# In-chunk scores as 64x64 blocks, the angle net padded to 128 rows, and VectorE's pairs of instructions joined, in a Mamba-like mixer with experts

## Chip, cores, metric

One core of a Trainium2 chip. The metric is the device time of one execution in microseconds (us), the median of the runs shown. All arithmetic is fp32. A run can be told from no change here when it differs by more than about 0.2%.

## What is computed

Input `x` is 8 sequences of 1024 tokens with 256 features. It is normalised (LayerNorm), and the result feeds a mixer and a layer of 8 experts (each token goes to one); both outputs are added to `x`. The mixer is a state-space scan with complex decay in chunks of tokens, cut to what matters here:

```python
theta = clip(theta_base + tanh(x @ theta_w1) @ theta_w2, -pi/2, pi/2)      # the "angle net"
lambda_eff = lambda_base + viscosity_eta * theta ** 2
log_z = complex(-lambda_eff * dt, theta * dt)                              # per head and state block
cumlog = cumsum(log_z, axis=1)                                             # within a chunk
A = where(t >= s, exp(cumlog[t] - cumlog[s]), 0)
S_total = exp(cumlog) * state + einsum('btshk,bshp->bthpk', A * B, x * dt)
y = einsum('bthk,bthpk->bthp', C, S_total).real                            # + x * D, gate, RMS norm, out projection
```

## The kernel before

A first part (to about 225 us) normalises, routes tokens to experts and runs the experts. The rest, which the change is about, is the mixer: `whole_mixer`, 32 macros of 256 tokens (`MACROS`, `MT`), each of 2 tiles of 128 tokens (`TPM`, index `ch`); a tile holds two chunks of 64 (`CH`). Four macros make one sequence.

The loops are unrolled, and the order of the work on each engine is written out by hand: each engine has one list of steps that runs three to five macros of `front_*` work (projections, angles, waves) ahead of the `back_*` work (scores, state, output). Engines meet through semaphores (`s["name"]`) only; each engine works its own list in order. The steps named later:

- TensorE: `front_x` and `front_z_a/b` project tokens through `project` (L900; `front_x` runs in even macros for two macros at once, 32 records in a row and 8 more); `front_theta` (L926) is the second layer of the angle net, K = 49 rows (48 hidden and a row of ones); `back_own` (L980) makes the scores of a tile, for 4 pairs `q` of heads and 2 heads `e` in a pair, each a block of 128x128 with K = 64; `back_cross` (L992) then overwrites the block that goes from the first chunk to the second, 64x64; `back_update` (L1005), `back_y_att` (L1016), `back_y_state` (L1027), `back_turn` and `front_turn` (L968, L956, transposes), `back_out` (L1036), `back_square_sum` (L1044).
- ScalarE: copies of projections from PSUM (`front_x`, L1130 and L1131), `front_lambda` (L1145, L1148), exponentials and sines, scaling of waves, seeds and copies for the back.
- VectorE: `front_conv` (L1380), `front_clip` (L1387, clips theta on its way out of PSUM), `front_angle`, `front_phase`, `front_decay` (L1418, a scan for each of 2 groups of 256 columns), `front_cin` (L1443, L1444) and `front_cown` (L1456, L1457), products of the replicated B or C rows with a wave, `back_mask` (L1477, causal mask on the scores of a tile), `back_state` (L1488), `back_gate` (L1498).

An fp32 matmul call shows as two MATMUL records in the trace, a transpose as one. A form such as 64*128 in a record is rows times columns of the array that the instruction takes.

## Time and profile before

| | |
|---|---|
| time, median of 3 runs | 1089.71 us (1088.63 to 1090.44) |
| profiled execution, span of its instructions | 1074.8 us (the profile states no other time of this execution) |
| TensorE matmul busy | 977.5 us, 91% |
| VectorE busy | 923.2 us, 86% |
| ScalarE busy | 853.5 us, 79% |
| GpSimd busy | 347.3 us, 32% |
| chain that ended last | TensorE 63%, ScalarE 7% |

The shares are of the whole span; the mixer's steady part is read from windows of its own. The median of the runs lies 14.9 us above the profiled span, time that the profile's instructions do not cover.

### The profile page before, as it was taken

The numbers are of one execution on the slowest core, as the hardware profiler recorded it, in microseconds if no ns is written. First come the engines' busy times: TensorE is split into PE (matmuls) and PEld (weight loads), VectorE is DVE, ScalarE is ACT, GpSimd is POOL, SyncE is SP. The second block draws the span as 40 slices with busy tenths as digits, with TensorE's granted clock in tenths as the row PEclk, the third lists the DMA queues.
The fourth block names the chain that finished last, engine by engine and source line by source line (L and its number), as shares of the span: only waits on it lengthen the run. The fifth ranks groups of instructions, "written<-read, shape, count | busy, mean of one in ns | idle before, by whom it ended". The sixth has DMA issues, their size and how long they took to land.

```text
span 1074.8 us, 25050 instructions
## 1 busy us (share of the span) xinstructions
PE 977.5 (91%) x8702; PEld 803.8 (75%) x8702; DVE 923.2 (86%) x1487; ACT 853.5 (79%) x1771; POOL 347.3 (32%) x347
## 2 busy tenths in 40 slices
PE   4972699876899999999999999999999999999995
PEld 2532477655688888888888888888888888888884
DVE  5859723259999999999999999999999999999971
ACT  3864212139789999999999999999999999999982
POOL 1210677400213343323222332322333333222332
PEclk9985699996899999999999999999999999999998
DMA  7969587614364665657575656656665657575662
GB/s 244 312 218 394 165 256 208 164 49 155 114 172 142 187 169 165 183 157 200 147 212 149 191 156 191 160 184 186 175 178 164 184 156 202 147 216 136 172 189 58
DMA packets 145986, 193.72 MB, mean 180 GB/s; under 512 B 16862, under 2 KB 106127, under 8 KB 144448
## 3 DMA queue, kind: packets, MB, share of 16 engines
q1 hardware_dynamic: 110656, 146.68, 41.0%
q0 software_dynamic: 24672, 34.36, 16.7%
q10 hardware_dynamic: 10528, 11.01, 3.0%
q8 instruction: 73, 1.20, 0.5%
q14 instruction: 57, 0.47, 0.1%
HBM read 75.99 MB, written 40.63 MB: 109 GB/s over the span
## 4 chain that ended last, share of the span: by engine, by line
PE 63%; ACT 7%; issue 4%; DVE 2%; POOL 2%; DMA 1%; ACTq 0%; POOLq 0%; DVEq 0%
PE ps L900 20%; PE ps L1036 9%; PE ps L980 6%; PE ps L1016 5%; PE ps L1027 5%; PE ps L1044 4%; PE ps L992 3%; PE ps L1005 3%; PE ps L968 3%; PE ps L956 3%; PE ps L926 2%; DVE conv L1380 1%; POOL plus_tile L1590 1%; ACT ps L1166 1%; DMA plus_tile<-x 1%
## 5 line engine op out<-in xcount | busy, mean ns | idle before, releaser
L900 PE MATMUL ps<-early,win 128*128 128x256 f32 x1152 | 275.2, 389 | 11.0 <-DVE theta L1387 6.8
L900 PEld LDWEIGHTS ps<-early,win 128*128 128x128 f32 x1152 | 213.9, 193 | 45.9 <-DVE theta L1387 7.2
L1380 DVE SCALAR_TENSOR_TENSOR conv<-x_pre,col,conv 128x512 f32<-128x512 f32 x240 | 162.6, 741 | 6.4 <-ACT conv L1131 6.3
L1590 POOL DMA_INDIRECT plus_tile<-expert_d,slot_of x64 | 95.7, 1495 | 170.2 <-DMA out<-plus_tile 100.8
L1612 POOL TENSOR_TENSOR rms<-ms,cst 128x1 f32<-128x1 f32 x64 | 52.0, 812 | 250.6 <-ACT ms L1244 250.5
L1036 PE MATMUL ps<-wout,g 128*128 128x256 f32 x512 | 122.9, 383 | 2.5 <-ACT o_tile L1253 2.2
L1036 PEld LDWEIGHTS ps<-wout,g 128*128 128x128 f32 x512 | 93.4, 190 | 18.9 <-issue 7.8
L1596 POOL DMA_DIRECT2D plus_tile<-x x64 | 60.9, 956 | 101.9 <-ACT plus_tile L1237 101.9
L551 POOL DMA_INDIRECT r_tiles<-xn_d,token_of x72 | 68.7, 954 | 71.1 <-POOLq L408 48.5
L1605 POOL DMA_DIRECT2D plus_tile<-o_tile x62 | 67.4, 1092 | 54.6 <-ACT o_tile L1253 42.6
L682 DVE TENSOR_TENSOR r_tiles<-ps,r_expw 128x256 f32<-128x256 f32 x72 | 25.5, 416 | 65.9 <-PE ps L569 63.0
L1477 DVE TENSOR_TENSOR att<-ps,cst 128x1024 f32<-128x1024 f32 x64 | 77.8, 1216 | 4.5 <-PE ps L992 4.5
L603 ACT ACTIVATE r_tiles<-ps 128x1024 f32<-128x1024 f32 x18 | 18.4, 1024 | 76.5 <-PE ps L560 76.5
L1166 ACT ACTIVATE ps<-xbc,col 128x128 f32<-128x128 f32 x256 | 79.2, 364 | 0.0
L1130 ACT ACTIVATE x_pre<-ps 128x512 f32<-128x512 f32 x80 | 47.7, 597 | 39.0 <-PE ps L900 38.9
L569 PE MATMUL ps<-r_expw,r_tiles 128*128 x288 | 71.7, 398 | 4.7 <-issue 4.5
L980 PE MATMUL ps<-cown_s,grow_s 64*128 64x128 f32 x1024 | 75.3, 287 | 0.0
L980 PEld LDWEIGHTS ps<-cown_s,grow_s 64*128 64x128 f32 x1024 | 62.9, 189 | 16.4 <-issue 15.3
L1016 PE MATMUL ps<-att,x_tok 128*64 128x128 f32 x1024 | 70.9, 281 | 3.4 <-DVE att L1477 3.4
L1027 PE MATMUL ps<-cin_s,state_in 64*64 64x128 f32 x1024 | 70.6, 277 | 0.0
L1044 PEld LDWEIGHTS ps<-cst,gsq 128*128 128x128 f32 x512 | 67.2, 192 | 3.3
L569 PEld LDWEIGHTS ps<-r_expw,r_tiles 128*128 128x128 f32 x288 | 53.4, 196 | 20.2 <-issue 14.1
(172 smaller groups left out, 2237.3 us busy)
## 6 DMA issues: line engine op xcount, KB each, us to landing
cin_s<-cin SPq DMA_DIRECT2D x64, 258.0 KB, 3.1
rep<-bc_d SPq DMA_DIRECT2D x128, 128.0 KB, 3.3
grow_s<-grow SPq DMA_DIRECT2D x64, 256.0 KB, 3.8
bup_s<-bup SPq DMA_DIRECT2D x64, 256.0 KB, 3.0
cown_s<-cown SPq DMA_DIRECT2D x64, 256.0 KB, 2.7
expert_d<-r_tiles ACTq DMA_DIRECT2D x18, 512.0 KB, 3.4
xn_d<-r_tokens SPq DMA_DIRECT2D x16, 512.0 KB, 4.3
xnT_d<-r_turned SPq DMA_DIRECT2D x4, 2048.0 KB, 24.1
```

The costliest lines, as they stand in the source:

```text
L551: pool.indirect_dma_start(e_in[b][:, t, :], None, xn_d, bass.IndirectOffsetOnAxis(ap=token_of[:, at:at + 1], axis=0)).then_inc(e_loaded[b] ...
L569: last = nc.tensor.matmul(e_Y[b][:, t // 2, (t % 2) * D_MODEL:(t % 2 + 1) * D_MODEL], e_xT[b][:, kt, t * P:(t + 1) * P], w8[:, bass.ds(e + ...
L900: last = nc.tensor.matmul(dst, win[:, kt, n * P:(n + 1) * P], xn_in[b][:, kt, :], start=(kt == 0), stop=(kt == KT - 1))
L980: last = nc.tensor.matmul(bank_s[:, e, q * P:(q + 1) * P], grow_s[b][both(e), place(q), here], cown_s[b][both(e), place(q), here], start=T ...
L1016: nc.tensor.matmul(bank_y[both(e), q * P:(q + 1) * P], x_tok[b][:, ch, own], att[ch][:, e * PAIRS + q, :], start=False, stop=False, skip_g ...
L1027: last = nc.tensor.matmul(bank_y[both(e), q * P:(q + 1) * P], state_in[ch][both(e), place(q), :], cin_s[b][both(e), place(q), here], start ...
L1036: nc.tensor.matmul(bank_o[:, 0:D_MODEL], g[ch][:, q, :], wout[:, q, :], start=(q == 0), stop=(q == PAIRS - 1))
L1044: last = nc.tensor.matmul(bank_o[:, D_MODEL:D_MODEL + 1], gsq[:, q, :], k("ones")[:, 0:1], start=(q == 0), stop=(q == PAIRS - 1))
L1166: last = nc.scalar.activation(bank_y[:, q * P:(q + 1) * P], xbc[m % XBC_BUFS][:, q, ch * P:(ch + 1) * P], ACT.Copy, scale=c("D", q))
L1380: nc.vector.scalar_tensor_tensor(conv[:, ct, :], x_pre[:, ct, tap:tap + PT], c("conv_w", ct * D_CONV + tap), conv[:, ct, :], ALU.mult, ALU ...
L1477: nc.vector.tensor_tensor(att[ch][:, :, :], bank_s[:, :, :].rearrange("p e (h t) -> p (e h) t", h=4), k("causal")[:, None, :].broadcast_to ...
L1590: pool.indirect_dma_start(plus_tile[m % 2][ch][:, :], None, expert_d, bass.IndirectOffsetOnAxis(ap=slot_of[:, t:t + 1], axis=0)).then_inc( ...
```

## The change

TensorE: `back_own` makes each chunk's own 64x64 block instead of a tile's whole 128x128 block: 16 calls with K = 64, 64 columns of weights and 64 moving columns, where there were 8 calls of 64x128x128. The quarter that nobody writes any more (second chunk to first) is zeroed once by a memset of VectorE before the mixer starts, and TensorE waits for it. Within a macro `back_update(m, 1)` moves ahead of `back_own(m + 1, 0)`. The angle net's weights get 79 rows of zeros, so that `front_theta` has K = 128. ScalarE gets a new step `front_theta_out` in each macro, which copies theta from PSUM to SBUF; `front_clip` then clips in SBUF. The two products of `front_cin` and of `front_cown` become one instruction each, the two scans of `front_decay` one.

```diff
-                    here = slice(ch * P, (ch + 1) * P)
+                    chunks = [slice(ch * P + n * CH, ch * P + (n + 1) * CH) for n in range(CPT)]
...
                     for q in range(PAIRS):
                         for e in range(2):
-                            last = nc.tensor.matmul(bank_s[:, e, q * P:(q + 1) * P], grow_s[b][both(e), place(q), here], cown_s[b][both(e), place(q), here], start=True, stop=True)
-                            if q == PAIRS - 1:
-                                last.then_inc(s["scored"], 1)
+                            for chunk, here in enumerate(chunks):
+                                last = nc.tensor.matmul(bank_s[both(chunk), e, q * P + chunk * CH:q * P + (chunk + 1) * CH], grow_s[b][both(e), place(q), here],
+                                                        cown_s[b][both(e), place(q), here], start=True, stop=True)
+                                if q == PAIRS - 1:
+                                    last.then_inc(s["scored"], 1)
...
-                pe.wait_ge(m_zero, 1)
+                pe.wait_ge(m_zero, 2)
...
                 for m in range(MACROS):
+                    back_update(m, 1)
                     back_own(m + 1, 0)
-                    back_update(m, 1)
...
+                def front_theta_out(m):
+                    after(act, s["lamsq"], m)
+                    after(act, s["angle"], m)
+                    act.wait_ge(s["thproj"], m + 1)
+                    nc.scalar.activation(theta[:, :, :], bank_b.rearrange("p (n t) -> p n t", n=GROUPS2), ACT.Copy).then_inc(theta_out, 1)
...
                     back_reseed(m + 2, 1)
+                    front_theta_out(m + 5)
                     front_x(m + 5, 4)
...
-                    after(dve, s["lamsq"], m)
-                    dve.wait_ge(s["thproj"], m + 1)
-                    nc.vector.tensor_scalar(theta[:, :, :], bank_b.rearrange("p (n t) -> p n t", n=GROUPS2), 0.25, -0.25, ALU.min, ALU.max).then_inc(s["clipped"], 1)
+                    dve.wait_ge(theta_out, m + 1)
+                    nc.vector.tensor_scalar(theta[:, :, :], theta[:, :, :], 0.25, -0.25, ALU.min, ALU.max).then_inc(s["clipped"], 1)
...
-                    for n in range(GROUPS2):
-                        nc.vector.tensor_tensor_scan(decay[:, n, :], k("restart"), lam[:, n, :], 0.0, ALU.mult, ALU.add).then_inc(s["rsum"], 1)
+                    flat = lam[:, :, :].rearrange("p g t -> p (g t)")
+                    nc.vector.tensor_tensor_scan(flat, k("restart"), flat, 0.0, ALU.mult, ALU.add).then_inc(s["rsum"], GROUPS2)
...
-                    nc.vector.tensor_tensor(prod[0][:, :, :, :], c_re, wave[:, :, :, :], ALU.mult).then_inc(s["cprod"], 1)
-                    nc.vector.tensor_tensor(prod[1][:, :, :, :], c_im, wave[:, :, :, :], ALU.mult).then_inc(s["cprod"], 1)
+                    waves = wave.rearrange("p r g t -> p (r g) t")[:, None, :, :].broadcast_to([P, 2, 2 * GROUPS2, MT])
+                    nc.vector.tensor_tensor(both_prods, c_rep, waves, ALU.mult).then_inc(s["cprod"], 2)
...
-                dve.wait_ge(m_zero, 1)
+                nc.vector.memset(bank_s[:, :, :], 0.0).then_inc(m_zero, 1)
+                dve.wait_ge(m_zero, 2)
```

`front_cown` changes as `front_cin` does; the waits of TensorE on `clipped` become waits on `theta_out`; `restart` is 512 columns wide instead of 256; the waits on `scored` count 6 for a tile instead of 4.

TensorE's list at the start of a macro's back, before (names are PSUM, weights and moving operands; `x8` is 8 calls):

```order
L900 MATMUL ps<-early,win 128x256 x4
L980 MATMUL ps<-cown_s,grow_s 128x128 x8
L1005 MATMUL ps<-x_tok,b_tok 64x64 x8
L992 MATMUL ps<-cin_s,bup_s 64x64 x8
L968 MATMUL ps<-cst,bup_s 128x128 x4
```

and the same place now:

```order
L902 MATMUL ps<-early,win 128x256 x4
L1009 MATMUL ps<-x_tok,b_tok 64x64 x8
L983 MATMUL ps<-cown_s,grow_s 64x64 x16
L996 MATMUL ps<-cin_s,bup_s 64x64 x8
L970 MATMUL ps<-cst,bup_s 128x128 x4
```

The scores of the chunks now stand beside the cross block, which has the same form of tile. ScalarE's list around the new copy (theta out of PSUM between the copy of the state and the last `front_x` column tile of an even macro), as it is now:

```order
L1156 ACTIVATE lam<-theta 128x512 [waits negd,expd,clipped]
L1159 ACTIVATE lam<-lam,col 128x256 [waits lamsq]
L1159 ACTIVATE lam<-lam,col 128x256
L1234 ACTIVATE ps<-state_in 128x256 [waits statein]
L1149 ACTIVATE theta<-ps 128x512 [waits thproj,angle,lamsq]
L1134 ACTIVATE x_pre<-ps 128x512 [waits xproj]
L1135 ACTIVATE conv<-ps,col 128x512
L1241 ACTIVATE b_tok<-ps 128x512 [waits upd,bturned]
```

Before, the row `theta<-ps` was not there, and the others followed in the same order. VectorE's list from the mask to the first scan, before:

```order
L1477 TENSOR_TENSOR att<-ps,cst 128x1024 [waits scored,yout]
L1402 TENSOR_TENSOR lam<-lam,early 128x512 [waits dt_loaded0,lamd]
L1387 TENSOR_SCALAR theta<-ps 128x512 [waits thproj,lamsq]
L1418 SCALAR_TENSOR_TENSOR lam<-cst,lam 128x256 [waits negd,expd,lamdt]
L1418 SCALAR_TENSOR_TENSOR lam<-cst,lam 128x256
L1395 TENSOR_TENSOR angle<-theta,early 128x512 [waits dt_loaded1,fracd,clipped]
```

and now, where the clip waits for ScalarE's copy (semaphore `cwave`, which is `theta_out`) and one scan stands for two:

```order
L1493 TENSOR_TENSOR att<-ps,cst 128x1024 [waits scored,yout]
L1418 TENSOR_TENSOR lam<-lam,early 128x512 [waits dt_loaded0,lamd]
L1403 TENSOR_SCALAR theta<-theta 128x512 [waits cwave]
L1434 SCALAR_TENSOR_TENSOR lam<-cst,lam 128x512 [waits expd,negd,lamdt]
L1411 TENSOR_TENSOR angle<-theta,early 128x512 [waits dt_loaded1,fracd,clipped]
```

The order of VectorE's steps is the same; each place has fewer rows.

## Rows read from the trace of the kernel before

**Rows 1.** Busy time of each engine by windows, clock and DMA

```profile
core 0: us, PE busy (x) PEld busy (x) DVE busy (x) ACT busy (x) POOL busy (x), PEclk, DMA share, GB/s
461.01:1015.08 554.07, 554.07 (x5458) 471.09 (x5458) 549.77 (x761) 524.68 (x1113) 174.66 (x176) 1.00 0.62 174
...
300.00:1041.00 741.00, 738.04 (x7316) 627.10 (x7312) 730.50 (x1005) 699.40 (x1489) 244.74 (x239) 1.00 0.62 174
225.00:300.00 75.00, 57.87 (x360) 46.25 (x361) 65.83 (x92) 59.05 (x104) 8.95 (x5) 0.82 0.32 106
1041.00:1064.00 23.00, 21.03 (x268) 18.48 (x268) 6.72 (x11) 9.14 (x24) 8.43 (x11) 1.00 0.44 110
```

**Rows 2.** The chain in order of time, two macros: start, length in us, piece

```profile
602.31 1.73 PE ps L900 x8
604.04 1.09 PE ps L980 x16
605.13 0.61 PE ps L1005 x16
605.74 0.61 PE ps L992 x16
...
609.46 1.02 PE ps L1016 x16
...
621.51 1.06 PE ps L926 x4
622.57 1.92 PE ps L900 x8
```

**Rows 3.** Waits from 461.01 to 1015.08: us in total, times, longest

```profile
ACT x_pre L1130 <- PE ps L900: 27.4, 33, 1.9
...
DVE g L1498 <- PE ps L1027: 4.3, 11, 0.5
```

**Rows 4.** VectorE groups by form, 461.01 to 1015.08: busy, mean ns, idle before

```profile
L1418 DVE TENSOR_TENSOR_SCAN lam<-cst,lam 128x256 f32<-128x256 f32 x44 | 27.7, 669 | 0.0
L1444 DVE TENSOR_TENSOR prod<-rep,wave 128x1024 f32<-128x1024 f32 x22 | 26.7, 1215 | 0.0
...
L1387 DVE TENSOR_SCALAR theta<-ps 128x512 f32<-128x512 f32 x22 | 15.0, 680 | 0.0
```

**Rows 5.** VectorE in order of time, steady part: start, length in us

```profile
608.00 1.22 DVE L1443 TENSOR_TENSOR prod<-rep,wave 128x1024 f32<-128x1024 f32 x1
609.13 1.22 DVE L1444 TENSOR_TENSOR prod<-rep,wave 128x1024 f32<-128x1024 f32 x1
610.27 0.68 DVE L1423 SCALAR_TENSOR_TENSOR frac<-frac,angle 128x512 f32<-128x512 f32 x1
```

**Rows 6.** VectorE groups by form, 60 to 130 us, the nearest to the new forms

```profile
L470 DVE TENSOR_TENSOR r_tokens<-r_tokens,r_route 128x2048 bf16<-128x2048 f32 x4 | 9.1, 2282 | 0.0
...
L446 DVE TENSOR_TENSOR_SCAN r_route<-cst,early 128x512 f32<-128x512 f32 x1 | 1.2, 1224 | 0.0
...
L641 DVE TENSOR_SCALAR early<-early 128x512 f32<-128x512 f32 x1 | 0.5, 489 | 0.8 <-ACT early L610 0.8
...
L642 DVE TENSOR_SCALAR early<-early 128x512 f32<-128x512 f32 x1 | 0.4, 426 | 0.0
```

**Rows 7.** ScalarE's copy of 512 columns from PSUM, groups by form, 461.01 to 1015.08

```profile
L1130 ACT ACTIVATE x_pre<-ps 128x512 f32<-128x512 f32 x55 | 32.8, 597 | 27.4 <-PE ps L900 27.4
```

**Rows 8.** Around theta's way out of PSUM, in order of time

```profile
623.80 0.37 ACT L1223 ACTIVATE ps<-state_in 128x256 f32<-128x256 f32 x1
...
626.04 0.68 DVE L1387 TENSOR_SCALAR theta<-ps 128x512 f32<-128x512 f32 x1
```

**Rows 9.** The mixer's start in order of time

```profile
224.37 0.27 DVE L1511 MEMSET state_in<- 128x256 f32 x1 [3.12 <-DMA expert_d<-r_tiles]
...
224.69 1.22 PE L1049 MATMUL ps<-state_in,cst 128*128 128x256 f32 x2
...
225.71 9.80 PE L900 MATMUL ps<-early,win 128*128 128x256 f32 x40
```

More of the change, by code:

```diff
@@ L43 @@
 CONST, _at = {}, 0
-for _n, _w in (("ident", P), ("minushalf", 8), ("causal", P), ("before", P), ("ones", P), ("restart", MT), ("tilestart", TILES * EXPERTS),
+for _n, _w in (("ident", P), ("minushalf", 8), ("causal", P), ("before", P), ("ones", P), ("restart", GROUPS2 * MT), ("tilestart", TILES * EXPERTS),
                ("first", EXPERTS), ("slot", SLOT_TILES), ("quarter", 1), ("halfpi", 1), ("eps", 1), ("ownhead", 2)):
@@ L101, in mixer_and_experts @@
         early_dt = [early[:, (XN_BUFS * KT + b * GROUPS2) * MT:(XN_BUFS * KT + (b + 1) * GROUPS2) * MT].rearrange("p (g t) -> p g t", g=GROUPS2) for b in range(2)]
-        early_hidden = [early_rows(XN_BUFS * KT + 2 * GROUPS2 + b, LORA + 1) for b in range(2)]
+        early_hidden = [early_rows(XN_BUFS * KT + 2 * GROUPS2 + b) for b in range(2)]
         passed = sem("passed")
@@ L672, in _ @@
                     for m in range(2):
-                        step(nc.vector.memset(early_hidden[m][32:LORA + 1, :], 1.0))
+                        step(nc.vector.memset(early_hidden[m], 1.0))
                     assert done[0] == ROUTE_READ
@@ L713, in whole_mixer @@
             trig, wave, grow, bpart, bup, cown = (wb(n, [P, 2, GROUPS2, MT]) for n in ("trig", "wave", "grow", "bpart", "bup", "cown"))
-            prod = [wb(f"prod{n}", [P, 2, GROUPS2, MT]) for n in range(2)]
+            prods = wb("prods", [P, 2, 2, GROUPS2, MT])
+            prod = [prods[:, n] for n in range(2)]
+            both_prods = prods.rearrange("p n r g t -> p n (r g) t")
             cin = wb("cin", [P, 2, GROUPS2, MT + TPM])
@@ L718, in whole_mixer @@
             rep = wb("rep", [P, 4, MT])
-            b_re, b_im, c_re, c_im = (rep[:, n:n + 1, None, :].broadcast_to([P, 2, GROUPS2, MT]) for n in range(4))
+            b_rep, c_rep = (rep[:, n:n + 2, None, :].broadcast_to([P, 2, 2 * GROUPS2, MT]) for n in (0, 2))
             hidden, xn_in, dt_in = early_hidden, early_xn, early_dt
@@ L738, in whole_mixer @@
             COPIES = 4 * 16
-            reseeded = s["wavedec"]
-            BEFORE = 4
+            reseeded, theta_out = s["wavedec"], s["cwave"]
+            SCORES = 6
             def place(q):
@@ L816, in stack_grow @@
                     b = m % 2
-                    after(sp, s["scored"], 8 * (m - 1))
+                    after(sp, s["scored"], TPM * SCORES * (m - 1))
                     sp.wait_ge(s["grown"], m + 1)
@@ L823, in stack_cin @@
                     b = m % 2
-                    after(sp, s["scored"], 8 * (m - 1))
+                    after(sp, s["scored"], TPM * SCORES * (m - 1))
                     after(sp, s["yout"], TPM * (m - 1))
@@ L833, in stack_bup @@
                     b = m % 2
-                    after(sp, s["scored"], 8 * (m - 1))
+                    after(sp, s["scored"], TPM * SCORES * (m - 1))
                     after(sp, s["bturned"], TPM * (m - 1))
@@ L841, in stack_cown @@
                     b = m % 2
-                    after(sp, s["scored"], 8 * (m - 1))
+                    after(sp, s["scored"], TPM * SCORES * (m - 1))
                     sp.wait_ge(s["cown"], 2 * (m + 1))
@@ L919, in front_theta @@
                     if m % 2:
-                        pe.wait_ge(s["clipped"], m)
+                        pe.wait_ge(theta_out, m)
                         after(pe, s["zevac"], 2 * (m - 1))
@@ L1138, in front_z @@
                     nc.scalar.activation(z_gate[b][:, 2 * h:2 * h + 2, :], (bank_a, bank_b)[h].rearrange("p (n t) -> p n t", n=2), ACT.Silu).then_inc(s["zevac"], 1)
+                @macro
+                def front_theta_out(m):
[3 more added lines that the diff above has]
+                    nc.scalar.activation(theta[:, :, :], bank_b.rearrange("p (n t) -> p n t", n=GROUPS2), ACT.Copy).then_inc(theta_out, 1)
                 @macro
@@ L1269, in scalar_mixer @@
                 front_x(0, 4)
+                front_theta_out(0)
                 front_z(0, 0)
                 front_lambda(0)
+                front_theta_out(1)
                 front_silu(0)
@@ L1295, in scalar_mixer @@
                 front_x(2, 4)
+                front_theta_out(2)
                 front_bpart(1, 1)
@@ L1308, in scalar_mixer @@
                 back_ms(0, 0)
+                front_theta_out(3)
                 front_trig(2)
@@ L1333, in scalar_mixer @@
                 back_b(1, 1)
+                front_theta_out(4)
                 front_x(4, 4)
```

14 lines of the change are left out of this document (7 added, 7 removed).

## Prediction

> **What bounds the kernel now.** I read the windows by stage first [rows 1]. From 461.01 to 1015.08 us, 11 repeats of a pair of macros and so 22 macros, TensorE is busy 554.07 of 554.07 us: 25.19 us a macro, at the full 2.4 GHz (granted clock 1.00). From 300 to 1041 it is busy 99.6%, with the same clock. So in these 741 us TensorE sets the pace, and the chain in order of time [rows 2] is one TensorE block behind another, with nothing between. Second, what the others need in the same 22 macros: VectorE 549.77 us (24.99 a macro), ScalarE 524.68 (23.85). The waits [rows 3] say where they stand idle: ScalarE 27.4 us before the copies of `front_x`, VectorE 4.3 before the gate, both for TensorE. VectorE is thus 0.2 us a macro behind the bound: whatever TensorE gains, VectorE lets through only 0.2 plus what it gains itself. That is the point on which the sum turns. Before 300 us and after 1041 VectorE and ScalarE are not full [rows 1].
>
> **TensorE, step by step.** Blocks in [rows 2] run from start to start, so they hold the cost of changing the form of tile. A projection of 8 records takes 1.73 us where the form before it is its own, 128*128, and 1.92 behind `front_theta`, whose form is 49*128; `front_theta` itself is 4 like records, so half of 1.73, 0.87, and takes 1.06. Entering and leaving costs 0.19 each time. With K = 128 its form is that of its neighbours: −0.38 a macro.
>
> `back_own` takes 1.09, `back_cross` 0.61. The length of a 64-column step follows from `back_y_att` (16 records, 128 moving columns, 1.02) against `back_update` (16 records, 64 columns, 0.61): 64 more columns cost 0.41 over 8 pairs of records, 0.051 a pair. So these tiles work two at a time, and a block of 8 pairs of 64 columns is 0.41, plus about 0.20 for the change of form. A projection of 256 columns at 0.216 a record gives 0.054 for 64 columns, the same step for a single tile.
>
> `back_own` now is 32 records of 64x64, in turn on the four quarters of the array. No row shows four quarters at once. Bounds: four at a time, 8 steps of 0.051, 0.41; two at a time, 0.82. Both pairings that it is built of are there: two row halves (`back_cross`) and two column halves (`back_update`) each reach 0.61 for 16 records, and nothing in the two looks like a limit that the other shares. I take 0.41, one step above the nearest rows, and keep 0.82. The block has the form of `back_cross` behind it, so the 0.20 is paid once for both. Own and cross together: 1.09 + 0.61 = 1.70 before, 0.41 + 0.61 = 1.02 now, −0.68, twice a macro −1.36 (two at a time: −0.54). The move of `back_update` is what puts own beside cross; it issues no DMA, and its own wait (copy of B, reseed) comes one block earlier, 1.09 us, where TensorE now never waits. TensorE needs 25.19 − 0.38 − 1.36 = 23.45 a macro (24.27 with two at a time).
>
> The Trainium skill, "TensorE: Matmul & The Clock Gate", section "Wait — 56ns, not 53.3ns?", says that matmuls never start less than about 25 ns apart however small they are. By it 32 records take 0.80 us, and the estimate for TensorE would be 24.2 us a macro instead of 23.45. The trace has a step of 0.051 for two records, so it neither reaches nor breaks that.
>
> **VectorE.** Records overlap: products follow each other at 1.13 and 1.14 us though each shows 1.22 [rows 5], so one costs its length less 0.08. The joined product has 2048 columns; the nearest row, 128x2048, is 2.28 [rows 6], so 2.20 against 2.27 for two: −0.07, and for both pairs −0.14. Bounds: no gain, if broadcasting reads cost something, and −0.16. Scans: two of 669 ns [rows 4] less the overlap are 1.18; one of 512 columns is 1224 ns [rows 6], 1.14: −0.04. Clip: 680 ns out of PSUM [rows 4]; in SBUF the rows with 512 columns are 426 and 489 ns [rows 6]: −0.25 or −0.19, I take −0.22. Sum −0.40: 24.99 becomes 24.59. It may be less, since "busy" counts short waits that lie under the overlap: up to 0.2 a macro, floor 24.4.
>
> **ScalarE.** One more copy of 512 columns out of PSUM, 597 ns [rows 7], 0.49 to 0.60 with and without the overlap: 23.85 becomes 24.34 to 24.45. Of its 27.4 us of waits, 1.25 a macro, nearly all stand in `front_x` and wait for TensorE, so they shrink as TensorE gets ahead. What is queued behind the copy: the last `front_x` evacuation, then `back_b`, the seed. The copy starts when the state copy before it is done: in the pair of [rows 2] that ends at 624.17 [rows 8], 1.6 us after `front_theta` (622.57), and VectorE reaches the clip at 626.04, 1.3 us after a copy of 0.6 would end. So I cost the new wait at nothing. If this cover went, each macro would lose up to the 0.6 of the copy.
>
> **Sum.** The slowest engine is VectorE with 24.59, ScalarE 0.15 to 0.25 behind, TensorE over 1 us ahead. I take a macro at 24.6: −0.59. The 741 us hold 29.4 macros: −17.3. Tail, TensorE busy 21.03 of 23.00 [rows 1], two tiles' scores: −1.4. Fill, 75 us, shared between three engines: −0.6 (0 to −2). Start: VectorE's new memset covers 1024 columns of PSUM; no such memset is there, one of 256 in SBUF takes 0.27 [rows 9], so 1.1, and TensorE's first projections wait for it since they start right after the first memset: +1.1 (0.5 to 1.3). Wider constants and weight rows: +0.3 (0 to 0.7). Together −17.9: span 1074.8 to 1056.9, and with the 14.9 us outside it (1089.71 − 1074.8) the median goes to 1071.8, say **1072**.
>
> **Rivals.**
> - *The quarters go two at a time, or by the 25 ns of the page.* TensorE then needs 24.2 to 24.3, all three engines lie within 0.35 of each other, and each one's waits cost the others: 24.75 a macro, −12.9 in the steady part, 1076. For it: no row has four at once. Against: the two pairings.
> - *Three engines full, poorly coupled.* VectorE 24.6 and ScalarE 24.4 wait for each other (exponentials to waves to scaling, convolution to SiLU to seed): a macro at 24.9 to 25.1, 1079 to 1087. For: between them only 0.15 to 0.25 us a macro is left, and both stand at 99% of such a period. Against: VectorE at 99% of TensorE's time costs TensorE nothing today.
> - *ScalarE becomes the bound and the kernel slower.* Its place: the copy ahead of the last `front_x` evacuation. If its present idle time stayed as it is (29.4 of 554 us, 1.34 a macro), it would need 23.85 + 0.5 + 1.34 = 25.7: +0.5 a macro, +15, about 1103. It decides from 0.85 us of idle that stays. Against: that idle time is waiting for TensorE.
> - *The quarters don't overlap at all*: 32 records at 0.051, 1.63, own and cross 2.24, +1.08 − 0.38 a macro: TensorE 25.9, 1110. Against: every form with two tiles overlaps.
> - *It does nothing*: VectorE's savings don't come (broadcast reads slow the joined products, the clip stays 0.6): period 24.9 to 25.1 again, at most −5.
>
> **Chances.** Forecast 0.55, with a range of its own from 1064 (VectorE at its floor 24.4: −23.2 − 1.4 − 2 + 1.1) to 1076; two at a time 0.15; poor coupling 0.15; nothing 0.05; ScalarE 0.06; no overlap 0.03; the small rest to both sides. The range goes to 1084, which takes in the second case and most of the third. Faster by over 0.2% (about what a measurement tells here) 0.87, within 0.2% 0.05, slower 0.08.
>
> **What would show it.** Own blocks of 32 records in about 0.41 to 0.45 us (0.8: two at a time), and 0.61 for cross behind them. `front_theta` 0.87 and 1.73 for what follows. TensorE idle for over 0.8 us a macro, waiting for masks, gates or copies of VectorE and ScalarE, and VectorE at 99% busy. Joined product near 2.28, scan 1.22, clip 0.43 to 0.49. The distance of two long projections, 50.37 us now for a pair of macros, at 49.2. ScalarE's waits in `front_x` down from 1.25 a macro to below 0.5. Clock 1.00: if TensorE's new gaps took it to 1.2 GHz for a stretch, or if ScalarE's list stood idle for VectorE and not for TensorE, the prediction is wrong.

## The result, and the profile after

The changed kernel takes **1097.93 us** (1097.24 to 1099.45) against 1089.76 us of the kernel before (four runs; the 1089.71 of the table further down is the median of three): a ratio of **1.0077, interval 1.0063 to 1.0092**. It is slower by 0.8%, where 1.6% faster was forecast. In short, the experiments below show two things: ScalarE, with the new copy in its list, sets the pace of the changed kernel, and once that copy is gone a VectorE without pauses holds up GpSimd's small operations, for which ScalarE waits.

The profiled execution took 1098.01 us with a span of 1096.2, so only 1.8 us lie outside the span. The page of after, its engines and the first line of its chain:

```profile
span 1096.2 us, 27099 instructions
...
PE 949.4 (87%) x9726; PEld 774.2 (71%) x9726; DVE 912.9 (83%) x1392; ACT 867.8 (79%) x1803; POOL 379.8 (35%) x347
...
ACT 41%; PE 16%; issue 16%; POOL 10%; DVE 3%; DMA 1%; another core or an unknown queue 1%; ACTq 1%; POOLq 0%; DVEq 0%
```

The chain has left TensorE. The windows that answer to [rows 1] (PE, PEld, DVE, ACT, POOL busy, clock, DMA share, GB/s):

```profile
461.01:1015.08 554.07, 531.15 (x6156) 451.17 (x6155) 541.56 (x693) 533.48 (x1133) 203.49 (x176) 1.00 0.63 175
...
225.00:300.00 75.00, 50.39 (x278) 39.11 (x278) 51.93 (x73) 44.64 (x79) 2.95 (x4) 0.82 0.29 90
1041.00:1064.00 23.00, 20.54 (x278) 17.77 (x278) 18.40 (x20) 21.28 (x51) 9.67 (x10) 1.00 0.74 199
```

In the steady part no engine is full now: TensorE idles 22.9 us, VectorE 12.5, ScalarE 20.6. The two later windows lie at other places of the program than in [rows 1], since everything runs later. GpSimd has gone up from 174.66 to 203.49 us with the same 176 instructions; the experiments come back to that.

The parts themselves came out nearly as costed. TensorE in order of time (start, length); what a block costs is the distance to the next start:

```profile
740.62 0.69 PE L983 MATMUL ps<-cown_s,grow_s 64*64 64x64 f32 x32
741.14 0.64 PE L996 MATMUL ps<-cin_s,bup_s 64*64 64x64 f32 x16
741.71 0.66 PE L970 MATMUL ps<-cst,bup_s 128*128 128x128 f32 x4
...
743.46 1.89 PE L902 MATMUL ps<-early,win 128*128 128x256 f32 x8
745.18 1.89 PE L1040 MATMUL ps<-wout,g 128*128 128x256 f32 x8
...
755.04 0.69 PE L983 MATMUL ps<-cown_s,grow_s 64*64 64x64 f32 x32
```

Own scores 0.52 and cross 0.57, 1.09 together where [rows 2] add up to 1.70; the projection behind the padded angle net 1.72 instead of 1.92. The four quarters do overlap: 32 records in 0.52 us are 16 ns apart on average. TensorE's busy time, 531.15 us or 24.1 a macro, is above the 23.6 that its blocks add up to with these lengths; some of them are longer behind a wait (the output projection 1.80 in the median instead of 1.73 from start to start), and the rest of the difference is not followed here. VectorE's and ScalarE's new forms in the steady part (busy, mean ns), which answer to [rows 4, 6, 7]:

```profile
L1460 DVE TENSOR_TENSOR prods<-rep,wave 128x2048 f32<-128x2048 f32 x22 | 50.2, 2282 | 0.0
...
L1434 DVE TENSOR_TENSOR_SCAN lam<-cst,lam 128x512 f32<-128x512 f32 x22 | 26.8, 1217 | 0.0
...
L1149 ACT ACTIVATE theta<-ps 128x512 f32<-128x512 f32 x22 | 12.7, 575 | 0.0
...
L1403 DVE TENSOR_SCALAR theta<-theta 128x512 f32<-128x512 f32 x22 | 9.2, 420 | 0.0
```

VectorE needs 541.56 / 22 = 24.62 us a macro (24.59 forecast; the window still holds 22 macros to within 0.2%, one pair of them a long one). All of this is close to the forecast, and yet the distance between two 32-record projections (`front_x` for ct 0 and 1, the clock of a pair of macros) fell only from 50.37 to 50.28 us. The waits say who held it. The third line is what the first of [rows 3] has become:

```profile
POOL rms L1629 <- ACT ms L1255: 168.2, 43, 6.7
...
PEld ps L1040 <- issue: 24.0, 32, 2.4
...
ACT x_pre L1134 <- PE ps L902: 17.0, 21, 1.6
PE ps L1040 <- ACT o_tile L1264: 15.5, 32, 2.1
```

TensorE waits at the output projection (L1040) for ScalarE's `o_tile`, the scaled output, and ScalarE, behind that, for the first `front_x` projection. So the two wait for each other in turn, a closed chain. The chain in order of time shows it; ScalarE works through some 40 us without a wait for another engine, of which the end is:

```profile
824.08 0.47 issue
...
826.30 1.28 ACT L1142
827.64 0.16 issue
827.90 0.19 issue
828.09 0.48 ACT o_tile L1264
828.70 1.97 PE ps L1040 x8
830.66 0.79 PE ps L1048 x8
831.45 1.06 PE ps L1020 x16
832.51 1.02 PE ps L1031 x16
833.53 0.61 PE ps L1009 x16
834.14 1.06 PE ps L902 x4
```

From the end of `o_tile` it is 5.6 us until TensorE starts the projection that ScalarE needs next, and meanwhile ScalarE runs out of work.

### The profile page after: what moved, and what is told of

Its sections match the earlier page's. It is cut to its first block, busy times and chain, and to the rows that moved or that the text cites. A ratio compares the mean times of both kernels' runs of the same rounds, so it can differ in the third digit from the quotient of the medians.

```text
span 1096.2 us, 27099 instructions
## 1 busy us (share of the span) xinstructions
PE 949.4 (87%) x9726; PEld 774.2 (71%) x9726; DVE 912.9 (83%) x1392; ACT 867.8 (79%) x1803; POOL 379.8 (35%) x347
## 4 chain that ended last, share of the span: by engine, by line
ACT 41%; PE 16%; issue 16%; POOL 10%; DVE 3%; DMA 1%; another core or an unknown queue 1%; ACTq 1%; POOLq 0%; DVEq 0%
POOL r_tiles L551 6%; PE ps L902 5%; ACT ps L1177 4%; ACT bup L1225 3%; PE ps L1040 3%; ACT L1142 3%; ACT conv L1135 3%; ACT L1210 2%; ACT x_tok L1186 2%; ACT bpart L1225 2%; PE ps L1020 2%; ACT plus_tile L1248 2%; ACT x_pre L1134 2%; ACT o_tile L1264 2%; PE ps L1031 2%
## 5 line engine op out<-in xcount | busy, mean ns | idle before, releaser
L902 PEld LDWEIGHTS ps<-early,win 128*128 128x128 f32 x1152 | 216.5, 194 | 43.6 <-DMA early<-xnT_d 5.7
L1607 POOL DMA_INDIRECT plus_tile<-expert_d,slot_of x64 | 110.4, 1726 | 162.1 <-DMA out<-plus_tile 85.0
L1629 POOL TENSOR_TENSOR rms<-ms,cst 128x1 f32<-128x1 f32 x64 | 69.6, 1088 | 239.6 <-ACT ms L1255 239.5
L1040 PE MATMUL ps<-wout,g 128*128 128x256 f32 x512 | 126.0, 389 | 27.0 <-ACT o_tile L1264 26.8
L1040 PEld LDWEIGHTS ps<-wout,g 128*128 128x128 f32 x512 | 94.2, 192 | 49.5 <-issue 38.1
L551 POOL DMA_INDIRECT r_tiles<-xn_d,token_of x72 | 69.0, 958 | 85.0 <-POOLq L408 48.5
L682 DVE TENSOR_TENSOR r_tiles<-ps,r_expw 128x256 f32<-128x256 f32 x72 | 25.5, 418 | 78.2 <-remote 50.2
L569 PE MATMUL ps<-r_expw,r_tiles 128*128 x288 | 74.4, 400 | 13.7 <-issue 12.1
L569 PEld LDWEIGHTS ps<-r_expw,r_tiles 128*128 128x128 f32 x288 | 49.2, 190 | 36.7 <-issue 33.0
L1460 DVE TENSOR_TENSOR prods<-rep,wave 128x2048 f32<-128x2048 f32 x32 | 73.1, 2284 | 0.0
L1473 DVE TENSOR_TENSOR prods<-rep,cin 128x2048 f32<-128x2048 f32 x32 | 73.0, 2282 | 0.0
```

Source lines behind the costliest of these rows:

```text
L551: pool.indirect_dma_start(e_in[b][:, t, :], None, xn_d, bass.IndirectOffsetOnAxis(ap=token_of[:, at:at + 1], axis=0)).then_inc(e_loaded[b] ...
L569: last = nc.tensor.matmul(e_Y[b][:, t // 2, (t % 2) * D_MODEL:(t % 2 + 1) * D_MODEL], e_xT[b][:, kt, t * P:(t + 1) * P], w8[:, bass.ds(e + ...
L902: last = nc.tensor.matmul(dst, win[:, kt, n * P:(n + 1) * P], xn_in[b][:, kt, :], start=(kt == 0), stop=(kt == KT - 1))
L1040: nc.tensor.matmul(bank_o[:, 0:D_MODEL], g[ch][:, q, :], wout[:, q, :], start=(q == 0), stop=(q == PAIRS - 1))
L1460: nc.vector.tensor_tensor(both_prods, c_rep, waves, ALU.mult).then_inc(s["cprod"], 2)
L1473: nc.vector.tensor_tensor(both_prods, b_rep, rotated, ALU.mult).then_inc(s["bprod"], 2)
```

## The experiments

There are fourteen runs beside the two kernels: the changed kernel once more (c1) and thirteen variants. Chips differ: the kernel before takes 1075.8 to 1076.7 us on four of them, and 1089 to 1090 in the first measurement and on one chip later, so ratios are each to the kernel before measured beside the run. The table gives them with the distances between the starts of the 32-record projections, read from TensorE's timeline: the intervals 2, 3 and 4 (the fill, in which the engines' lists are only getting under way; interval 1 lies between 29.6 us in e2 and 33.7 in e3 and isn't shown), then the usual later interval, and the longer ones. The intervals are those of the one profiled execution, while the times are medians, and where long pairs come and go the two can differ: e1's executions run from 1070.48 to 1084.96 us with 1083.62 profiled, e3's from 1063.92 to 1078.41 with 1073.84, e8's from 1069.40 to 1080.45 with 1069.50.

| kernel | us | ratio [interval] | intervals 2, 3, 4 | steady | longer ones |
|---|---|---|---|---|---|
| before | 1089.71 | 1 | 48.4, 52.0, 52.0 | 50.37 | none |
| changed | 1097.93 | 1.0077 [1.0063, 1.0092] | 55.4, 53.2, 52.0 | 50.28 | 52.09 |
| c1 changed again | 1085.15 | 1.0081 [1.0065, 1.0098] | 54.9, 53.3, 52.0 | 50.29 | 52.08 |
| e1 no copy | 1077.26 | 1.0009 [0.9983, 1.0035] | 45.8, 53.0, 49.3 | 49.31 | 53.86, three of 54.95 |
| e2 copy alone | 1084.64 | 1.0077 [1.0061, 1.0093] | 56.6, 52.2, 52.2 | 50.37 | 52.15 |
| e3 TensorE's part alone | 1076.81 | 0.9992 [0.9969, 1.0014] | 45.9, 49.1, 50.0 | 49.88 | 57.17 |
| e4 VectorE's joins alone | 1076.82 | 1.001 [1.0001, 1.002] | 48.5, 53.0, 51.8 | 50.37 | none |
| e5 changed, theta 2 early | 1080.86 | 1.0041 [1.0026, 1.0055] | 50.2, 53.2, 52.0 | 50.29 | 53.74 |
| e6 e1 + 2 memsets | 1068.37 | 0.993 [0.9916, 0.9943] | 46.9, 49.0, 49.6 | 49.55 | 55.93 |
| e7 e1 + 4 memsets | 1062.78 | 0.9866 [0.9849, 0.9882] | 45.9, 49.0, 49.8 | 49.65 | 53.55 |
| e8 e5 + 4 memsets | 1072.42 | 0.9975 [0.9956, 0.9995] | 48.6, 49.9, 50.3 | 50.29 | none |
| e9 before + 4 memsets | 1075.5 | 0.999 [0.9973, 1.0007] | 50.1, 52.1, 50.4 | 50.37 | none |
| e10 e3 + 4 memsets | 1071.38 | 0.9942 [0.9919, 0.9964] | 46.0, 49.0, 50.2 | 50.0 | 55.49 |
| e11 e7 + 2 memsets | 1075.59 | 0.987 [0.9852, 0.9888] | 45.6, 53.1, 49.3 | 49.68 | none |
| e12 e8, ScalarE relieved | 1072.9 | 0.985 [0.9836, 0.9864] | 49.7, 49.3, 49.4 | 49.42 | none |
| e13 e7 + 2 others | 1061.59 | 0.9863 [0.9839, 0.9886] | 45.7, 49.0, 49.7 | 49.7 | none |

### The change taken apart: e1 to e4

e1 is the changed kernel with the theta copy undone; e2 to e4 each put one part alone into the kernel before.

```diff
 # e1, against the changed kernel
 def front_clip(m):
-    dve.wait_ge(theta_out, m + 1)
-    nc.vector.tensor_scalar(theta, theta, 0.25, -0.25, ALU.min, ALU.max)
+    after(dve, s["lamsq"], m)
+    dve.wait_ge(s["thproj"], m + 1)
+    nc.vector.tensor_scalar(theta, bank_b, 0.25, -0.25, ALU.min, ALU.max)
 # and no front_theta_out in ScalarE's list; TensorE waits for s["clipped"] again
 # e2: before + copy. e3: before + 64x64 own, padding, moved update, bank memset.
 # e4: before + joined products and scan
```

> The changed kernel without ScalarE's copy of theta: VectorE clips out of PSUM again, the rest of the change stays. Theory (a closed chain through ScalarE and TensorE sets the steady period, and the copy is what filled it): the distance of two 32-record projections falls from 50.28 us to 49.0 to 49.5, ScalarE's busy time in 22 macros falls by 10 to 13 us, and the time is 1084 to 1090 us. Rival (the copy is hidden, and something else of the change holds the period, VectorE or the order of TensorE): distance stays at 50.2 to 50.4, time 1097 to 1100. In both, the mixer's start (the first 40-record projection) shows whether the later start of the changed kernel belongs to the copy: neither theory says so, so 237 to 239 us.

> The kernel before with ScalarE's copy of theta and the clip in SBUF alone. Theory: TensorE still needs 25.19 us a macro, ScalarE's chain gets 0.48 us a macro longer and just reaches it: distance 50.3 to 50.9, time 1090 to 1102 us. Rival (the copy is hidden in ScalarE's wait for TensorE): distance 50.37 unchanged and 1088 to 1091 us.

> The kernel before with TensorE's part alone: own scores as 64x64 blocks, the angle net padded, the state update moved ahead, the memset of the bank. Theory: ScalarE's chain is as before and has about 1 us a pair of slack, VectorE needs 49.98 us a pair: distance 49.9 to 50.1, steady part 3 to 5 us shorter, time 1086 to 1091. Rival (the move of the state update or the mixed tile forms make TensorE wait anew): distance 50.3 or more, time above 1092. If the late start of the mixer comes with this part (128-row weights and memset of the angle net's tiles), it shows here at about 238 us, otherwise at about 226.

> The kernel before with VectorE's joined products and scan alone. Theory: VectorE is 0.2 us a macro behind the bound, so no gain in the steady part (distance 50.37), 1088 to 1091 us. Rival (a joined instruction ends later than the first of a pair did, and the waves, copies or exponentials behind it wait): distance over 50.5, time above 1093.

The copy alone costs as much as the whole change (e2: 1.0077, the change: 1.0077), but taking it away gives no gain either (e1: 1.0009), although its steady distance is **49.31 us, where 49.2 was forecast**. Of e2 the theory had the size right and the place wrong: its distance stays 50.37, as the rival said, and 5.2 us are lost in the fill (its third long projection starts at 311.75 us instead of 306.53). e3 has 49.88 with VectorE at 544.8 of 545 us, as expected, but one pair of 57.17. e4 gains nothing, as expected. So two things take the gain away: something in the fill that belongs to the copy, and single long pairs that appear when the copy is gone.

**The long pairs.** In e1 TensorE and ScalarE both wait in such a pair. ScalarE waits for GpSimd's power (`back_rms`, which raises the mean square of each token to a power for the norm: one element per partition). From 606 to 623 us, GpSimd:

```profile
606.13 3.31 POOL L1595 DMA_INDIRECT plus_tile<-expert_d,slot_of  x1 [0.30 <-issue]
611.44 9.65 POOL L1617 TENSOR_TENSOR rms<-ms,cst 128x1 f32<-128x1 f32 x1 [2.00 <-ACT ms L1248]
622.29 0.93 POOL L1601 DMA_DIRECT2D plus_tile<-x  x1 [1.20 <-ACT plus_tile L1241]
```

and VectorE beside it:

```profile
611.17 0.46 DVE L1492 TENSOR_TENSOR state_in<-ps,cin_s 128x256 f32<-128x256 f32 x1
611.51 0.72 DVE L1467 TENSOR_TENSOR cown<-prods 128x512 f32<-128x512 f32 x1
612.11 0.73 DVE L1468 TENSOR_TENSOR cown<-prods 128x512 f32<-128x512 f32 x1
612.71 4.10 DVE L1384 SCALAR_TENSOR_TENSOR conv<-x_pre,col,conv 128x512 f32<-128x512 f32 x6
616.68 0.73 DVE L1473 TENSOR_TENSOR bup<-bup,bpart 128x512 f32<-128x512 f32 x1
617.28 0.73 DVE L1474 TENSOR_TENSOR bup<-bup,bpart 128x512 f32<-128x512 f32 x1
617.88 2.78 DVE L1384 SCALAR_TENSOR_TENSOR conv<-x_pre,col,conv 128x512 f32<-128x512 f32 x4
620.53 1.26 DVE L1481 TENSOR_TENSOR att<-ps,cst 128x1024 f32<-128x1024 f32 x1
```

The power takes 0.55 us where nothing holds it up. Here it takes 9.65 and ends 0.56 us after the mask has started, which is its normal length from there on. Between lie 14 VectorE instructions in 9.0 us, every one with two SBUF inputs, back to back; the mask is the first that has one of its two from PSUM. In e3 the same stretch holds up one of GpSimd's gathers (an indirect DMA that it issues to fetch a tile's expert rows), 9.74 us instead of 1.1, and ScalarE waits 7.5 us for its rows:

```profile
407.91 9.74 POOL L1594 DMA_INDIRECT plus_tile<-expert_d,slot_of  x1 [0.18 <-issue]
```

It ends 1.06 us after the mask starts (416.59), again its normal length. I call this a lockout. It is no novelty of the change: in the trace of before a gather issued at 384.78 us, in the fill, takes 4.83 and ends 0.97 after the start of the gate (388.64), which reads PSUM; the pair around it takes 52.0 us.

The Trainium skill, "SBUF — State Buffer", section "SBUF: two separate sides", says that a VectorE instruction with two SBUF inputs and a GpSimd instruction that reads SBUF exclude each other on a shared port pair, the one that starts first keeping it for its whole instruction while the other is blocked. The traces fit that, and go further: the block lasted over 14 instructions, not one, and the same instructions held up gathers too.

### The fill, and the chip: c1 and e5

Where is the time of the fill lost? In the trace of after, ScalarE and then VectorE around the copy for macro 2:

```profile
285.20 0.57 ACT L1241 ACTIVATE b_tok<-ps 128x512 f32<-128x512 f32 x1
286.59 0.60 ACT L1241 ACTIVATE b_tok<-ps 128x512 f32<-128x512 f32 x1 [0.81 <-PE ps L970]
287.08 0.59 ACT L1134 ACTIVATE x_pre<-ps 128x512 f32<-128x512 f32 x1
287.56 0.78 ACT L1135 ACTIVATE conv<-ps,col 128x512 f32<-128x512 f32 x1
288.22 0.61 ACT L1149 ACTIVATE theta<-ps 128x512 f32<-128x512 f32 x1
```

```profile
281.17 2.72 DVE L1397 SCALAR_TENSOR_TENSOR conv<-x_pre,col,conv 128x512 f32<-128x512 f32 x4
288.86 0.43 DVE L1403 TENSOR_SCALAR theta<-theta 128x512 f32<-128x512 f32 x1 [4.97 <-ACT theta L1149]
```

TensorE's product, theta of macro 2, is there at 282.7. ScalarE does exponentials, two B copies and a `front_x` evacuation first, VectorE waits 4.97 us, and behind the waiting clip stand the waves of macro 1 and the first mask, for which TensorE waits. e5 moves the one line; c1 is the changed kernel unaltered. Both ran on the same chip.

```diff
                 front_trig(1)
+                front_theta_out(2)
                 front_exp(1)
                 back_b(0, 0)
                 back_b(0, 1)
                 front_x(2, 4)
-                front_theta_out(2)
```

> The changed kernel once more, unaltered, beside the others on their chip. On another chip the kernel before took 1075.8 us where it had taken 1089.7, and the trace of the changed kernel came from the slower one. Theory (the mixer's start at 237.99 us instead of 225.71 belongs to that chip and its expert stage, not to the change): here the first 40-record projection starts at 224 to 227 us if this chip is the faster kind, and the ratio to the kernel before is again 1.006 to 1.009. Rival (the late start belongs to the change, through its wider weights or its code): 237 us whatever the chip, and a ratio of 1.015 or more on a fast chip.

> The changed kernel with one line of ScalarE's list moved: in the fill the copy of theta for macro 2 stands ahead of the exponentials of macro 1 instead of behind them, two B copies and the last front_x. Theory (the loss is in the fill: VectorE's clip waits 5.0 us for this copy, with the waves of macro 1 and the first mask queued behind it): the second interval of the 32-record projections shrinks from 55.35 to about 50 us, the steady part stays at 50.28, and the time is 4 to 6 us below that of the changed kernel, within 2 us of the kernel before or up to 0.2% under it. Rival (the wait is covered, ScalarE is late anyway): under 1 us less than the changed kernel.

e5: interval 2 goes from 54.86 to 50.17 and the time is 4.3 us down, as the theory said; but it stays 4.9 us above the kernel before, where at most 2 had been expected. In c1 the mixer's first projections start here:

```profile
227.15 1.06 PE L902 MATMUL ps<-early,win 128*128 128x256 f32 x2
```

against 237.99 in the first trace of the same code: those 11 us are not the change's but the chip's. From the first memset to this projection it is 2.47 us (224.68 to 227.15), in [rows 9] 1.34: the memset of the bank, 0.91 us, costs 1.1. The other 0.3 us by which c1 starts later lie ahead of it, where executions differ anyway (e5 has the same memset and starts at 223.75).

### GpSimd let in: e6, e7, e9, e10

If the block is VectorE's unbroken run, an instruction without SBUF inputs inside it should end it. These kernels add memsets of one column to VectorE's list (`open_port`), which write a tile that nobody reads.

```diff
+def open_port(m):
+    nc.vector.memset(port[:, opened.pop()], 0.0)     # a new column each time
 # in VectorE's loop over m
     front_cin(m + 2)
+    open_port(m)          # e7 to e13 only
     front_frac(m + 3)
     ...
     front_conv(m + 4, 0, 6)
+    open_port(m)
     front_bup(m + 2)
     back_join(m, 1)
+    open_port(m)
     front_conv(m + 4, 6, 10)
     ...
     front_decay(m + 3)
+    open_port(m)          # e7 to e13 only
```

> The changed kernel without ScalarE's copy (as in the first experiment), plus two memsets of one column that VectorE does inside its run of state, sums, convolution and B products. In the first experiment the distance of two long projections was 49.31 us, as forecast, but every third pair took 54.95, and in these GpSimd's power for the norm, a single element per partition, took 9.65 us: from the start of that run of VectorE instructions with two SBUF operands to the first one that reads PSUM, the mask. Theory (VectorE, never idle now, locks GpSimd out while it runs instructions with two SBUF operands back to back; an instruction with none lets it in): the power never takes over 5.3 us, the 54.95 us pairs are gone or cost under 2 us, distance 49.4, time 1058 to 1066 us where the kernel before takes 1075.8. Rival 1 (one column is too short to let GpSimd in): the power still takes 9.6 us and the time stays at 1070 to 1085. Rival 2 (the long power is only a symptom and the stall has another cause, a late transfer): the powers get shorter and the 54.95 us pairs stay.

> As the port-gap experiment, with two more one-column memsets of VectorE in each macro: behind the scan, ahead of the last five steps of the convolution, and behind the joined product of C, ahead of the fractions. With two memsets the power once took 5.65 us (the run of scan, convolution, angle) and a gather 5.1 and 3.3, and that pair was 55.93 us long. Theory (lockout, ended by any instruction without two SBUF operands): no power or gather above 4.5 us, all pairs 49.3 to 49.7, time 1060 to 1064 us beside 1075.9. Rival (the stall that is left is not from the lockout): one or two pairs of 55 us stay, time 1067 to 1070.

> The kernel before with the four one-column memsets a macro and nothing else, as a control. Theory (before, TensorE is the bound and VectorE's own waits let GpSimd in): distance 50.37, time within 0.15% of the kernel before. Rival (the memsets or the openings help by themselves, and the gain of the port-gap experiment isn't the change's): over 2 us faster.

> The kernel before with TensorE's part (64x64 own blocks, padded angle net, update moved ahead, memset of the bank) and the four memsets, without VectorE's joins and without ScalarE's copy. Alone, that part had a steady distance of 49.88 us (VectorE busy 544.8 of 545 us) and no gain: in its trace a gather of GpSimd's took 9.74 us and the pair with it 57.17. Theory: the long pairs go, the steady distance stays at 49.8 to 49.9 (VectorE's need without the joins), 1063 to 1067 us. Rival (lockout isn't what cost it): a pair of 55 us or more stays and the time is above 1071.

By the ratios e6 is 0.79%, 8.5 us, faster than e1, to which it adds the memsets alone; its 1068.37 us miss the 1058 to 1066 that had been expected. The 9.65 us powers are gone; the first two memsets don't lie in the run of scan, convolution and angle, and there a power still takes long, over its bound of 5.3:

```profile
666.62 5.65 POOL L1625 TENSOR_TENSOR rms<-ms,cst 128x1 f32<-128x1 f32 x1 [3.37 <-ACT ms L1250]
672.45 5.12 POOL L1603 DMA_INDIRECT plus_tile<-expert_d,slot_of  x1 [0.18 <-issue]
```

It ends 0.5 us after the gate (which reads PSUM) starts at 671.77, with the 55.93 us pair behind it. With four memsets (e7) no power of the mixer takes over 1.7 us (two gathers, at 286.06 and 424.55 us, still take 5.96 and 4.97, where 4.5 was the bound) and the time is **1062.78, ratio 0.9866**. Its steady part is the one that was forecast, with VectorE as the bound. Its row for 461 to 1000 us:

```profile
461.00:1000.00 539.00, 521.86 (x6095) 445.82 (x6093) 539.00 (x774) 519.97 (x1100) 193.45 (x175) 1.00 0.63 176
```

The price of the memsets is 49.65 − 49.31 = 0.34 us a pair for eight. The control e9 shows that they give the kernel before nothing that this measurement can tell: there TensorE is the bound. e10 gains 0.6%, but its median and the pair of 55.49 in its profiled execution are what the rival named. In that pair a gather takes 7.10 us, from 410.12: it starts behind the state's product, runs through the first, unopened part of the stretch above, isn't ended by the memset at 414.99, and ends 1.0 us behind the one at 416.21. So it looks like the same block, in a part of the list where the memsets came too late, and one memset isn't sure to let a gather in.

### ScalarE's part in the steady distance: e8 and e12

> The whole changed kernel (ScalarE's copy of theta included), with the copy for macro 2 moved ahead in the fill and the four one-column memsets a macro. Theory: the copy keeps ScalarE's closed chain at 50.28 us a pair, so the memsets save only the one long pair (1.8 to 3.5 us): distance 50.28, no pair above 51, 1077 to 1079 us. Rival (GpSimd's lockout, and not ScalarE's list, holds the steady pair at 50.28): distance 49.5 to 49.9 and 1066 to 1072 us.

> The changed kernel with its copy, with the early theta copy and the four memsets, and ScalarE relieved at another place: its scaling of the gathered expert rows covers one column instead of 256 (so the gate is left out of the other 255 columns), twice a macro, some 0.25 us less each, 1.0 us a pair. Theory (ScalarE's list, a closed chain with TensorE's projections, holds the pair at 50.29 us): the distance falls to 49.4 to 49.7, to VectorE's need, and the time by 6 to 9 us against 1072.4. Rival (not ScalarE's load but the new dependence holds it, projection to copy to clip, or the freeing of the bank): distance stays at 50.2 to 50.3, time within 2 us of 1072.4.

```diff
 # e12, against e8
-nc.scalar.activation(tile[:, :], tile[:, :], ACT.Copy, scale=gate[:, t:t + 1])
+nc.scalar.activation(tile[:, 0:1], tile[:, 0:1], ACT.Copy, scale=gate[:, t:t + 1])
```

e12 leaves out the gate for 255 of the 256 columns, so its output is not the mixer's: it serves to weigh ScalarE's list and is no version to use.

e8: the distance stays at 50.29, so GpSimd doesn't hold the changed kernel's steady pair. I had expected the memsets to save one long pair only; by the ratios (1.0041 to 0.9975) they saved 0.66%, 7.1 us, against e5, and intervals 3 and 4 of the fill (53.24 and 52.0) also fell, to 49.94 and 50.30. Those look like lockouts as well: in e5 these two hold a gather of 4.33 us and three powers of 2.35 to 2.53, in e8 none of the powers takes over 1.2 and no gather over 2.6. But the profiled execution of e8 is one of its fastest, so the median may hold long pairs that the table doesn't show.

e12 makes ScalarE's four scalings a pair shorter (minimum, median and maximum in ns, e8 and then e12):

```profile
L1250 ACT ACTIVATE plus_tile<-plus_tile,gate x44: 500/512/538, 463.2 to 995.4; 128x256 f32<-128x256 f32 x44
L1250 ACT ACTIVATE plus_tile<-plus_tile,gate x43: 281/298/326, 477.3 to 993.6; 128x1 f32<-128x1 f32 x43
```

That is 4 x 0.214 = 0.86 us, and the distance falls by 50.29 − 49.42 = 0.87. Copy and dependences are the same, and in e8 none of these scalings waits for its rows. **ScalarE's list sets the changed kernel's pair.** That the two agree to 0.01 us says less than it seems, since VectorE is at 99.5% in e12 and would soon have stopped the fall. The time fell by more than the 6 to 9 us that were expected: 1.25% by the ratios, 13 us, of which the shorter pairs explain some 11. The row of e12, from 475 to 1011 us:

```profile
475.00:1011.00 536.00, 522.49 (x6114) 444.65 (x6112) 533.56 (x772) 518.65 (x1120) 175.09 (x175) 1.00 0.63 178
```

### The last long pair: e11 and e13

```diff
 # e11, against e7: inside the convolution
-front_conv(m + 4, 0, 6)
+front_conv(m + 4, 0, 3); open_port(m); front_conv(m + 4, 3, 6)
-front_conv(m + 4, 10, 15)
+front_conv(m + 4, 10, 13); open_port(m); front_conv(m + 4, 13, 15)
 # e13, against e7: between gate, phase and waves
     back_gate(m + 1, 1)
+    open_port(m)
     front_phase(m + 4)
+    open_port(m)
     front_waves(m + 3)
```

> The version with four memsets and without the copy, with two more: inside the first six steps of the convolution and inside its last five. What was left there: one pair of 53.55 us in the fill, where a gather took 4.97 us and the power behind it was late. Theory (lockout): no pair above 51 us, steady distance 49.7 (0.1 more for four memsets a pair of 0.03 to 0.05 each), time 1059 to 1062 where the four-memset version has 1062.8. Rival (the late gather has another cause, its queue or its transfer): the 53 us pair stays and the time is 1063.

> The version with four memsets and without the copy, with two more memsets in the one long run that neither it nor the six-memset version opened: between the gate and the phase scan, and between the phase scan and the waves. In the traces of both, the one long pair that was left (53.55 and 53.09 us) has a late GpSimd instruction exactly there: a gather of 4.97 us that ends 1 us behind the start of the mask, and a power of 3.03 us that ends 0.5 us behind it. Theory (lockout): no pair above 51.5 us, time 3 to 4 us below the four-memset version less 1 us for the memsets: a ratio to the kernel before of 0.983 to 0.985 where that version has 0.9866. Rival (that pair is long for the ramp of the fill, and GpSimd's late instruction only falls into it): the 53 us pair stays, ratio 0.987.

e11 opened the wrong run: a pair of 53.09 us stays, with a power of 3.03 us between gate and mask, where no memset stood, and the ratio is e7's. e13 opens that run, and in its profiled execution no pair is above 49.89 us and no power above 1.7. But its median ratio, 0.9863, can't be told from 0.9866, and 0.983 to 0.985 had been expected. That the last long pair is a lockout is likely from where it stands and from its absence in e13; what it is worth in the median stays open.

e13 and e7 are faster than both kernels: 1.3 to 1.4% under the kernel before, 2.1% under the changed one by the ratios.

## Why the prediction was wrong, point by point

Between the kernel before (1075.92) and the changed one (1085.15) lie 9.2 us on one chip. From the starts in c1 and in the trace of before, whose profiled execution was of the same kind of chip: start +1.4, interval 1 −1.7, interval 2 +6.4, interval 3 +1.3, steady −0.8, one long pair +1.7, tail +0.4; together 8.7. The forecast had −17.3 for the steady part, and its −0.8 is the larger share of the miss: there ScalarE's list holds the pair (e8, e12), and where the copy is gone, GpSimd's lockout takes back what the shorter pair gains (e1, e6, e7). Behind the plus signs the experiments put two causes: the place of one copy in the fill (4.3 us, e5) and the lockout (7.1 us, e8 against e5). The two needn't add up to 9.2, since the kernel before has lockouts in its fill too, and the memsets take away more than the change brought. With both mended the change is worth −0.25%; without the copy and with GpSimd let in, −1.34%, 14.4 us.

- **TensorE, own and cross 1.02: 1.09 measured**, mis-sized by 0.07. The rival of two at a time falls with 16 ns a record. So does the floor of 25 ns in the Trainium skill, "TensorE: Matmul & The Clock Gate", section "Wait — 56ns, not 53.3ns?", for records on different quarters of the array. `front_theta` came close to its cost: 0.97 us behind a short wait, 0.87 without one (in e7), and 1.72 for what follows.
- **VectorE 24.59 a macro: 24.62 measured.** Products and scan came within 10 ns of the rows chosen for them, the clip at 420 ns where 460 was taken.
- **"I cost the new wait at nothing": the first step that failed.** The cover, the time by which the copy is done before VectorE gets to the clip, was read at one place, in the steady part (1.3 us there), and not in the fill, which has a list of its own. There the clip waits 4.97 us with waves and mask behind it, and moving that one copy gives back 4.3 us (e5).
- **"They shrink as TensorE gets ahead": the second, and the one that cost the steady gain.** ScalarE's waits for projections went from 27.4 to 17.0 us, 0.77 a macro where below 0.5 was forecast, and 20.6 / 22 = 0.94 us a macro of idle time stayed. The rival "ScalarE becomes the bound" named the copy, and a point of decision at 0.85 us of idle that stays: 24.25 busy + 0.94 idle = 25.19. It had 6 in 100. It had the engine right, but not the price or the place: the idle it was to keep whole (1.34) shrank by a third, so the steady pair didn't get longer, and the loss against the kernel before lies in the fill. What the prediction missed is that waiting for TensorE can itself be a result of ScalarE's lateness: TensorE waited at L1040 for `o_tile`. That only shows when the chain is followed around. The experiments bear it out: with ScalarE's list 0.86 us shorter the pair is 0.87 shorter (e12), and without the copy it is 49.31 (e1).
- **Not in any rival: GpSimd.** The sum compared three engines that were to be full at once and left out the fourth, 32% busy. A full VectorE locks it out, and ScalarE waits for it: 9.65 us instead of 0.55 in e1, and its pair takes 54.95 instead of 49.31. The rival "three engines full, poorly coupled" had the right symptom and the wrong place. This is also why e1, whose steady distance came out within 0.1 us of the forecast, gained nothing.
- **The base.** I took 14.9 us as lying outside the span, from a median of 1089.71 and a span of 1074.8. Each run here is its span plus 1.8 us; so the trace of before, with its 1074.8, must be of a faster kind of chip than the median (its mixer starts at 225.71 us, as those of the faster chips do). That didn't change the sign of the forecast, but the 14.9 us are no time outside a span.
- **Start +1.1: right.** From the first memset to the first long projection it is 1.1 us more (2.47 against 1.34). **Tail −1.4: +0.4 measured**; what took it was not tested.

## What to carry to other kernels

When the bound is taken away and VectorE gets full, look at who lives in VectorE's pauses. Here GpSimd's small operations and its gathers needed one, and four one-column memsets a macro between VectorE's instructions with two SBUF inputs cost 0.04 us each and were worth 1.4% (e1 to e7). An engine's idle time is free only if the wait behind it isn't caused by that engine itself: follow the chain once around before loading it. And where the fill has a list of its own, an operation moved to another engine has to be placed there by itself, counting what is queued behind its reader.

## What was not expected of the hardware

- GpSimd's one-element power, 0.55 us, took 9.65 us beside 14 VectorE instructions with two SBUF inputs, and ended 0.5 to 0.6 us after the first instruction with an input from PSUM began (three cases: 9.65 us in e1, 5.65 in e6 and 3.03 in e11). Gathers of 9.74 us in e3, 4.97 in e7 and 4.83 in the kernel before ended 1.0 to 1.1 us after such a start. Memsets of 0.06 us, which have no input, took most of these blocks away (e6, e7), though not each of them ended one (e10). Not every power in such a run was held for all of it: in e1 one issued at 562.13 us took 1.56. What lets it in there is open, and so is why only every third pair was struck. Powers of 1.3 to 1.9 us stand in many pairs, in the kernel before too (1.35 us in most of its pairs).
- Lateness can multiply: in the long pair of c1 TensorE waited 2.06 us for `o_tile`, the granted clock of 600 to 605 us was 0.76, so part of it at 1.2 GHz, and the output projection behind the wait took 3.65 us instead of 1.97.
- The same code took about 1076 us on some chips and 1089 on others, the changed kernel 1085.15 and 1097.93. Of these 12.8 us 10.8 lie ahead of the mixer, which starts at 223.5 to 227.2 us on the ones and at 238 to 240 on the others.
